# Retention sums from max(x, 0), on GpSimd and in the bank of the value product

## The reference, cut to what matters

```python
qk = jnp.einsum('bhqd,bhkd->bhqk', qr, kr) * mask[None]      # 4 x 16 heads, 1024 x 1024, causal decay mask
denom = jax.lax.stop_gradient(jnp.clip(jnp.sum(jnp.abs(qk), axis=-1, keepdims=True), 1.0, 50000.0))
out = jnp.einsum('bhqk,bhkd->bhqd', qk / denom, vr)           # D = 8 columns a head
```

## Time and profile before

| | us |
|---|---|
| median of three runs | 1021.5 |
| lowest and highest | 1019.57, 1024.63 |
| span of the profiled execution, first to last instruction | 1008.0 |
| PE busy | 874.2 (87%) |
| DVE busy | 816.2 (81%) |
| ACT busy | 725.7 (72%) |
| POOL busy | 289.1 (29%) |

### The profile page before, as it was taken

The page is one execution under the profiler, slowest core; times in us unless marked ns, Lnnn a source line. Parts: engine busy times, 40 slices in busy tenths (PEclk is TensorE's granted clock), DMA queues, the critical chain, the costliest instruction groups (busy, mean ns, idle before and its releaser), DMA issues. The chain is left out here.

```text
span 1008.0 us, 25094 instructions
## 1 busy us (share of the span) xinstructions
PE 874.2 (87%) x9373; PEld 464.7 (46%) x9374; DVE 816.2 (81%) x1699; ACT 725.7 (72%) x1493; POOL 289.1 (29%) x331
## 2 busy tenths in 40 slices
PE   4999899899999999999898898778999999979960
PEld 3666543334333333333344666533444444458850
DVE  6665499899999999999923766589999999928895
ACT  2666408788888888888784454478999999948851
POOL 4865311111111000000003656500344443005560
PEclk9999859999999999999999888768999999989995
DMA  5579851644445353330004899695354643546637
GB/s 167 223 267 331 280 133 42 205 101 105 110 98 125 89 123 84 68 69 14 13 24 127 277 317 301 226 241 101 67 118 94 114 89 54 136 142 189 206 119 252
DMA packets 121560, 147.20 MB, mean 146 GB/s; under 512 B 19213, under 2 KB 81242, under 8 KB 120800
## 3 DMA queue, kind: packets, MB, share of 16 engines
q1 hardware_dynamic: 116064, 133.74, 48.0%
q0 software_dynamic: 5376, 11.85, 4.1%
HBM read 77.63 MB, written 69.54 MB: 146 GB/s over the span
## 5 line engine op out<-in xcount | busy, mean ns | idle before, releaser
L854 ACT ACTIVATE probsB<-psB 128x512 f32<-128x512 f32 (+2 forms) x640 | 310.0, 566 | 87.1 <-PE psB L928 61.5
L766 DVE TENSOR_REDUCE mxB<-psB 128x1 f32<-128x512 f32 (+2 forms) x448 | 256.9, 642 | 11.1 <-PE psB L892 8.3
L921 PE MATMUL psB<-q_groups,k_groups 64*128 64x512 bf16 (+3 forms) x768 | 205.8, 330 | 16.6 <-DVE mxB L766 8.3
L892 PE MATMUL psB<-k_groups,q_groups 64*128 64x512 bf16 (+3 forms) x768 | 217.0, 344 | 2.8 <-PEq L293 1.7
L959 PE MATMUL psB<-probsB,vB 128*32 128x512 f32 (+3 forms) x1536 | 164.5, 500 | 0.7 <-ACT probsB L854 0.5
L1725 ACT ACTIVATE psD<-psD 128x896 f32<-128x896 f32 (+2 forms) x192 | 153.4, 799 | 12.9 <-PE psD L1779 12.7
L921 PEld LDWEIGHTS psB<-q_groups,k_groups 64*128 64x128 bf16 x768 | 67.5, 94 | 161.2 <-ACT probsB L854 140.3
L1656 DVE TENSOR_REDUCE sumsD<-psD 128x1 f32<-128x128 f32 (+3 forms) x256 | 113.2, 481 | 11.8 <-PE psD L1802 9.4
L899 PE MATMUL psB<-hideB,chooseB 64*128 64x128 bf16 (+1 forms) x1024 | 115.1, 210 | 0.0
L1779 PE MATMUL psD<-k_groups,q_groups 64*128 64x512 bf16 (+3 forms) x384 | 104.4, 343 | 12.3 <-ACT psD L1725 5.6
L766 DVE TENSOR_REDUCE mx2B<-psB 128x1 f32<-128x384 f32 (+2 forms) x192 | 104.4, 594 | 8.5 <-PE psB L899 6.9
(11 more groups left out here) (227 smaller groups left out, 1504.5 us busy)
## 6 DMA issues: line engine op xcount, KB each, us to landing
v<-vaugA SPq DMA_DIRECT2D x4, 2048.0 KB, 8.9
vB<-v SPq DMA_DIRECT2D x16, 512.0 KB
q_groups<-q SPq DMA_DIRECT2D x32, 200.0 KB
k_groups<-k SPq DMA_DIRECT2D x32, 200.0 KB
q_groups<-q SPq DMA_DIRECT2D x32, 192.0 KB
k_groups<-k SPq DMA_DIRECT2D x32, 192.0 KB
back<-emptyB POOLq DMA_DIRECT2D x16, 256.0 KB, 3.8
o<-outB SPq DMA_DIRECT2D x128, 32.0 KB, 1.8
```

The source lines that it names most:

```text
L766: nc.vector.tensor_reduce(dst, src, AX.X, ALU.max).then_inc(max_read, 1)
L854: nc.scalar.activation(probs[:, n % DEEP, 0:w], st[n % BANKS][:, 0:w], ACT.Exp, scale=DH ** -0.5).then_inc(exp_done, 1)
L892: ins = nc.tensor.matmul(bank[:, to:to + w], q[half[r], s, hq // 2, t * P:t * P + P], k[half[r], s, hq // 2, HALF * c:HALF * c + w], start ...
L921: ins = nc.tensor.matmul(bank[:, to:to + w], k[half[r], s, hq // 2, jt * P:jt * P + P], q[half[r], s, hq // 2, i0:i0 + w], start=True, sto ...
```

## The change

The sum of magnitudes is written as the sum of |x| = 2 max(x, 0) - x. The values are laid out with nine columns a head, the ninth -1, so the value product yields the minus sum as well. The max of a pair of tiles, 1,024 columns, is one instruction: on POOL for the first three pairs of a group, on ACT for the last. PE multiplies it with a column of twos and adds it to the same rows of the same bank (`add_above`, which takes the place of `diagonal_sums`). With nine rows for each of two tiles, four pairs fill one bank, so ACT copies and SP stores once a group. POOL spreads the values into the new layout. DVE's and ACT's magnitudes go, and DVE sums two equal score blocks of a piece in one instruction.

```diff
+    PAIRS = NT * NQ // 2
+    PAIRS_OF = NT // 2
     AHEAD = 4
     COUNT_AT = 2 * SLOTS_D
-    FIRST_SCATTER, SCATTERS = 3, 6
+    FIRST_SCATTER = 3
+    OUT_ROWS = DH + 1
+    PITCH = 2 * OUT_ROWS
+    SCATTERS_BEHIND = (1, 2, 1, 2)
...
-        po, pd = ps[:, 7, 0:2 * P], ps[:, 7, 2 * P:4 * P]
+        po = ps[:, 7, :]
...
+        twos = m.sb("twosD", [P, 2, VW])
...
+        v_rows = m.sb("v_rowsD", [P, 2, NT, D])
+        v = m.sb("vD", [P, 2, NT * H * PITCH + VW])
...
+        out = m.sb("outD", [P, GROUPS_KEPT, HALF])
+        above = m.sb("aboveD", [P, 2 * PAIRS_HELD, 4 * P])
...
+        def wait_above(engine, pair):
+            g, j = divmod(pair, PAIRS_OF)
+            engine.wait_ge(above_pool, (PAIRS_OF - 1) * g + min(j + 1, PAIRS_OF - 1))
+            if j == PAIRS_OF - 1 or g:
+                engine.wait_ge(above_act, g + (1 if j == PAIRS_OF - 1 else 0))
...
+                    sp.wait_ge(out_kept, g + 1)
+                    for hq in range(4):
+                        sp.dma_start(A["o1"][b, 4 * s + hq].rearrange("d (j r i) -> r d j i", j=PAIRS_OF, r=2),
+                                     out[VW * hq:VW * hq + PITCH, g % GROUPS_KEPT, :].rearrange("p (j i) -> p j i", i=P)
+                                     ).then_inc(out_stored[g % 2], 16)
...
+                    if len(units) == 2 and units[0][1] == units[1][1]:
+                        (hq, t), (other, _) = units
                         unit = 4 * (t - 1) + hq
-                        ins = V.tensor_reduce(sums[:, s, unit:unit + 1], src[:, at:at + P * t], AX.X, ALU.add,
+                        ins = V.tensor_reduce(sums[:, s, unit:unit + other - hq + 1:other - hq],
+                                              src[:, 0:2 * P * t].rearrange("p (a i) -> p a i", a=2), AX.X, ALU.add,
...
-                        if first % NT < 6:
-                            dve.wait_ge(abs_act, 3 * ((first - DEEP) // NT) + first % NT // 2 + 1)
+                        wait_above(dve, (first - DEEP) // 2)
...
-                        for t in {3: (1,), 7: (3,), 12: (5,), 16: (6, 7)}.get(i, ()):
-                            magnitude(NT * g + t)
...
+                def clear_values(i):
+                    nc.gpsimd.memset(v[:, i, :], 0.0).then_inc(cleared, 1)
+                    pool.wait_ge(cleared, 2 * i + 1)
+                    nc.gpsimd.memset(v[:, i, 0:NT * H * PITCH].rearrange("p (g c) -> p g c", c=PITCH)[:, :, PITCH - 1],
+                                     -1.0).then_inc(cleared, 1)
...
+                def spread_values(b):
+                    i = b % 2
+                    pool.wait_ge(v_loaded[i], 16 * (b // 2 + 1))
+                    if b >= 2:
+                        pool.wait_ge(po_done, NT * QUADS * (b - 1))
+                    pool.wait_ge(cleared, 2 * i + 2)
+                    nc.gpsimd.tensor_copy(v[:, i, 0:NT * H * PITCH].rearrange("p (g c) -> p g c", c=PITCH)[:, :, OUT_ROWS:OUT_ROWS + DH],
+                                          v_rows[:, i].rearrange("p t (h d) -> p (t h) d", d=DH)).then_inc(v_spread, 1)
...
-                label_rows()
-                for i in range(2 * NT * B):
-                    pool.wait_ge(piece_read, PIECES * FIRST_SCATTER + PIECES // SCATTERS * i + 1)
-                    scatter(i)
+                def keep_above(pair):
+                    pool.wait_ge(piece_read, masked_at(pair))
+                    if pair >= PAIRS_HELD:
+                        pool.wait_ge(above_added, pair - PAIRS_HELD + 1)
+                    tiles, held = 2 * pair % DEEP, 2 * (pair % PAIRS_HELD)
+                    nc.gpsimd.tensor_scalar(above[:, held:held + 2, :], kept[:, tiles:tiles + 2, :], LARGEST, 0.0,
+                                            ALU.min, ALU.max).then_inc(above_pool, 1)
...
+                pool.wait_ge(kept_until.x1_stored, 32 * B + 1)
+                clear_values(0)
+                spread_values(0)
+                kept_until.wait_second(pool)
+                clear_values(1)
+                sent = 0
+                for pair in range(PAIRS):
+                    g, j = divmod(pair, PAIRS_OF)
+                    if j < PAIRS_OF - 1:
+                        keep_above(pair)
+                    if j == 1 and g % QUADS == 1 and g // QUADS + 1 < B:
+                        spread_values(g // QUADS + 1)
+                    if g == FIRST_SCATTER and j == 0:
+                        label_rows()
+                    if g >= FIRST_SCATTER:
+                        for _ in range(min(SCATTERS_BEHIND[j], 2 * NT * B - sent)):
+                            scatter(sent)
+                            sent += 1
                 pool.wait_ge(scattered, 16 * 2 * NT * B)
...
+                def keep_group(g):
+                    if g == 0:
...
+                    if g >= GROUPS_KEPT:
+                        act.wait_ge(out_stored[g % 2], 64 * (g // 2))
+                    act.wait_ge(above_added, PAIRS_OF * (g + 1))
+                    nc.scalar.copy(out[:, g % GROUPS_KEPT, :], po).then_inc(out_kept, 1)
...
+                def keep_above(pair):
+                    act.wait_ge(piece_read, masked_at(pair))
+                    if pair >= PAIRS_HELD:
+                        act.wait_ge(above_added, pair - PAIRS_HELD + 1)
+                    tiles, held = 2 * pair % DEEP, 2 * (pair % PAIRS_HELD)
+                    nc.scalar.activation(above[:, held:held + 2, :], kept[:, tiles:tiles + 2, :], ACT.Relu).then_inc(above_act, 1)
...
-                    if j in (3, 6, 9):
-                        magnitude(NT * g + 2 * (j // 3 - 1))
-                    if beat > AHEAD and (beat - AHEAD) % 3 == 1:
-                        keep_bank((beat - AHEAD) // 3)
-                for n in range((SLOTS_D * NQ - AHEAD + 1) // 3, BANKS + 1):
-                    keep_bank(n)
+                    if beat >= SLOTS_D and j == 0:
+                        keep_above(PAIRS_OF * g - 1)
+                    if beat >= SLOTS_D and j == AHEAD - 1:
+                        keep_group(g - 1)
+                keep_above(PAIRS - 1)
+                keep_group(NQ - 1)
...
+                def inside(pair):
+                    g, j = divmod(pair, PAIRS_OF)
+                    b, s = divmod(g, QUADS)
+                    if s == 0 and j == 0:
+                        pe.wait_ge(v_spread, b + 1)
+                    pe.wait_ge(piece_read, masked_at(pair))
+                    if j == 0 and g:
+                        pe.wait_ge(out_kept, g)
+                    for r in range(2):
+                        t = 2 * j + r
+                        for hq in range(4):
+                            at = (t * H + 4 * s + hq) * PITCH + OUT_ROWS * (1 - r)
+                            ins = nc.tensor.matmul(po[VW * hq:VW * hq + VW, P * j:P * j + P], v[:, b % 2, at:at + VW],
+                                                   kept[:, (2 * pair + r) % DEEP, P * hq:P * hq + P], start=(r == 0), stop=False,
+                                                   skip_group_check=True)
+                        ins.then_inc(po_done, 1)
+
+                def add_above(pair):
+                    j = pair % PAIRS_OF
                     if pair == 0:
-                        g, later = divmod(group, 2)
-                        pe.wait_ge(abs_act, 3 * g + (3 if later else 2))
-                        pe.wait_ge(abs_dve, 5 * g + (5 if later else 2))
-                    if n == BANKS:
-                        pe.wait_ge(bank_kept, n)
-                    for i in range(4):
-                        ins = nc.tensor.matmul(pd[VW * i:VW * i + VW, :], ones[:, :],
-                                               absd[:, (4 * group + i) % DEEP_ABS, 2 * P * pair:2 * P * pair + 2 * P],
-                                               start=True, stop=True)
-                    ins.then_inc(bank_done, 1)
+                        pe.wait_ge(cleared_twos, 3)
+                    wait_above(pe, pair)
+                    for r in range(2):
+                        for hq in range(4):
+                            ins = nc.tensor.matmul(po[VW * hq:VW * hq + VW, P * j:P * j + P], twos[:, r, :],
+                                                   above[:, 2 * (pair % PAIRS_HELD) + r, P * hq:P * hq + P], start=False,
+                                                   stop=(r == 1), skip_group_check=True)
+                    ins.then_inc(above_added, 1)
 
...
+                    for dst, src in ((inter[:, i, :], A["inter"][b]), (intra[:, i, :], A["o1"][b, :, 0:DH, :]),
+                                     (diag[:, i, :], A["o1"][b, :, DH, :].rearrange("h (t i) -> h t i", i=P)),
                                      (sums[:, i].rearrange("p q u h -> p q (u h)"), A["sums"][b].rearrange("q p u -> p q u")),
                                      (gate1[:, i], A["g1"][b].rearrange("p (t c) -> p t c", c=D)))[part]:
                         sp.dma_start(dst, src).then_inc(side_in[i], 16)
```

More of the change, by code:

```diff
@@ L51 @@
 MASKED = -1.0e30
+LARGEST = float(np.finfo(np.float32).max)
 MAGNITUDE = 0x7FFFFFFF
```

(66 more changed lines are left out.)

88 lines of the change are left out of this document (22 added, 66 removed).

## The result

The changed kernel takes 1063.55 us (median of 4, 1062.13 to 1063.94) against 1020.54 us for the kernel before (4, 1016.81 to 1024.63): ratio 1.042, 95% interval 1.039 to 1.046. The forecast was 1007.4 us, its range 1001 to 1033. The change costs 43 us where 14 were to be saved.

The account below looks back on a forecast made before the run. ACT was taken to set the steady group at 13.34 us, DVE close behind. Steady groups -13.5, start +2.5, later spreading copies +1.0, groups 1 and 2 -2.4 and end -1.7 gave -14.1 us: 1007.4 us, range 1001 to 1033.

Parts of the forecast that it names:

- Groups 3 to 15: Retention stage, steady groups: each falls from 13.34 to 12.3 us, -13.5 us over 13 groups.
- in-order coupling: ACT idling behind PE, which serves ACT and DVE in order: 0.9 us a group on top of ACT's 11.42.
- POOL full: Rival 1, groups with scatters: POOL needs 13.2 us with a maximum at 1.85; 1020.8 us in all, chance 0.20.
- POOL decides: Rival 2, PE waiting for POOL at the sums: maximum 2.2 us, POOL 14.3 a group; 1035.5 us in all, chance 0.24.
- K: POOL's max of 1,024 columns, three a group: taken as 1.2 us, with ends at 1.1 and 2.2.
- Rival 3: PE's 10.6 us can't be packed between two consumers: groups take 12.9 us, 1015.2 us in all, chance 0.12.
- First groups: Groups 1 and 2, where DVE sheds 1.86 us each: 1.2 each taken, -2.4 us (0 to -3.7).
- The 2.5 us that I put on the start: Stage start: POOL's spreading copy and first sums waiting for the maximum add 2.5 us (0 to 6).
- End: Stage end, from the last score to the next stage's first ACT instruction: 8.3 us becomes about 6.6, -1.7.
- The other 13.5 lie outside the span: Profiled span 1008.0 us against the runs' median 1021.5: the 13.5 us between lie outside the span and stay.

Follow-up runs that it names:

- e4: Changed kernel with its 64 scatters left out: 1017.22 us, 0.996 of the kernel before.
- e7: Changed kernel without scatters, and with ACT's copy of the bank one beat earlier: 1002.69 us, 0.990 of the kernel before.
- e13: Kernel before with three maxima of 1,024 columns a group added on POOL, each right ahead of a scatter, on data nobody else reads: 1.016.
- e16: Kernel before with three maxima of 8 columns a group added on POOL, each right ahead of a scatter: 1.001.
- e18: Changed kernel with POOL's maxima shrunk from 1,024 to 8 columns from the second group on: 1.037 of the kernel before.
- e2: Kernel before, its six scatters a group waiting for the pieces at which the changed kernel issues them: 1.006.
- e12: Changed kernel with its three POOL maxima a group on DVE and the scatters waiting for every third piece: 1.009 of the kernel before.
- e14: Changed kernel with POOL's maxima on DVE, scatters every third piece, and ACT's copy one beat earlier: 1.007 of the kernel before.
- second profile: Kernel before, unchanged, profiled once more: groups of 13.34 to 13.35 us from group 4 on, no product late.
- e8: Changed kernel with a plain store of the same rows from POOL's queue replacing each scatter: 1010.28 us in one run, kernel before 1012.12.
- e17: Changed kernel with plain stores in place of the scatters and ACT's copy one beat earlier: 0.988 of the kernel before.
- e3: Kernel before with POOL also waiting, before each scatter, for PE's semaphore of the sums at a count reached long before: 1.001.
- e10: Kernel before with POOL also waiting, before each scatter, on a DVE semaphore at a count reached long before: one run, groups 13.4 us.

## Why the prediction was wrong

**The step that failed.** "Groups 3 to 15: 13 x (13.34 - 12.3) = -13.5." The ten groups with six scatters took 17.8. Of these 5.5 us too much, 4.5 come with the scatters, that is from PE's late reports and the lower clock with them (17.8 against 13.3 in e4; 4.0 against all ten groups of e4, its three at a lower clock included), 0.7 from the copy (13.3 against 12.62 in e7), and 0.3 is the rest of the in-order coupling. The prediction gave a scatter a price on one engine, 1.27 us of POOL's time, and none elsewhere. In the rows of before that was all it had: with or without scatters, 13.34. The price elsewhere came with the new order: a maximum ahead is one way (e13, e16), and the order of the changed kernel brings it without a full maximum too (e18).

**Why it costs so much here.** This part is argued and not shown. The kernel before has ACT full, 13.34 of 13.34; the changed kernel has no full engine, and its group is a chain of handovers between PE, ACT and DVE with two score buffers, in which a late report can move all that follows. For it: with maxima and scatters on POOL a group grows by 2.3 us in the kernel before (e13) and by 4.5 in the changed one. But a second cause lies beside it: the reports are also later in the changed kernel, up to 3.36 us against 1.98 for the longest in e13. And a full engine is no sure cover, since e2 and e13 slow the kernel before, ACT's 13.34 us notwithstanding. The new form of the product alone is not it: e12 and e14 have that form beside scatters, and lose under 0.1 and 0.8 us a group to them.

**Rivals 1 and 2: POOL full, POOL decides.** Both fail by their price. K takes 1.03 us (median of 48), below my 1.2 and far from 1.85 and 2.2; POOL is busy for 9.0 us of a group. PE's sums waited for POOL's maxima 3.2 us in the whole stage, 1.3 of it at the first one. The time came out beyond my range, on rival 2's side, with POOL idle half of the time. The Trainium skill, GPSIMD Engine Reference, section 4.1, has one-input work at "roughly line-rate"; K at 1.0 ns a column agrees. The prediction's estimate of 1.85 us from its section 7, which is on kernels written for GpSimd's own cores, does not fit this instruction.

**Rival 3: PE in order.** Alone, without the scatters, it would have been the nearest: 12.9 us a group forecast, 13.3 measured in e4. My 0.9 us of coupling was 1.7 (13.30 less ACT's 11.59), 0.7 of which was one place that I had named, the product behind the copy. I had priced that wait from ACT's side, 0.7 us of idle time, as part of the 0.9, and left the copy where it stood.

**Right.** ACT 11.42, measured 11.6; DVE 11.04, measured 11.2 to 12.0; eight matmuls of 128 columns for four of 256 cost nothing (0.64 us busy either way); masks stayed at 680 ns; spreading copies 1.16 for 1.2. First groups: 54.9 us for three against 57.0 in the first profile, though 59.5 in the second, so the executions differ by more than the 2.4 us forecast. The 2.5 us that I put on the start don't show: the first group took 20.0 us against 20.4 and 20.7. End: 6.5 us from the last score to the table load, 6.6 forecast, 8.3 before.

**A wrong statement.** "The other 13.5 lie outside the span." The spans that came with the later runs lie 1.6 to 1.9 us below their times in all kernels. The profile before had caught an execution 12 us shorter than the median. Of that, 4.8 us lie in this stage's first four groups (57.0 and 13.3 us, against 59.5 and 15.6 in the second profile); the later groups don't differ. The sum was taken off the median, so the number didn't suffer.

## What to carry to other kernels

When a change takes work off the engine that is full, ask what that engine may have been hiding, and look at every slow or irregular neighbour again, above all at indirect DMAs from GpSimd; leave the transfers out once, in both kernels, and see what they cost in each. Before moving elementwise work to GpSimd beside indirect DMAs, time the two together, with the semaphores of the other engines in view, not only GpSimd's busy time. And where an engine in order waits for one copy a group, try that copy a beat earlier first: here it was 0.7 us of 13.3.

## What the runs showed of the hardware

PE's semaphore updates can come up to 2.7 us late while indirect DMAs are being issued on GpSimd, and several then land within 0.3 us. Its matmuls' starts go on meanwhile for over a microsecond, not to the end: in the example above 13 of a value product's 16 start by 799.4 us, the last three at 799.78. With late reports there is a gap behind a scatter's start: of the updates of PE in this stage 79 come 0.9 to 1.3 us after a scatter's start in the kernel before and 87 in e16, but 19 in the changed kernel and 15 in e13; each has 64 scatters, and 5, 5, 20 and 36 of its 673 updates are missing. In e12 the gap lies at 0.5 to 0.9 us (10, against 68 in the kernel before). Plain stores of the same size from the same queue never did this (e8, e17: no product over 1.12 us, PE's slow clock included). The Trainium skill, SBUF — State Buffer, section "Who interferes with whom", says that "DMA never contends with a compute engine". For plain stores the traces agree; for the reports of PE beside indirect ones they don't, though its subject is ports, and no run here shows which path is blocked. What makes one program free of it (before, e16) and another not (e3, e10), with scatters at nearly the same times, stays open; distance between scatters doesn't settle it, since scatters 1.9 us apart are harmless in the first two and late in the others.
